# Inverse transform of two channels at a time, a second buffer for shifted rows, and the bias of three convolutions as one bf16 product

## What is computed

```python
xf = jnp.fft.fft2(x)                                  # per channel, 128x128
out_cplx = attention_of_heads(xf) @ xf                # out_f = abs(ifft2(out_cplx))
g = sigmoid(conv1x1(relu(bn(conv1x1(xf.real)))))
out_f_l = jnp.abs(jnp.fft.ifft2(g * xf))
fsa = conv1x1(concat([out_f, out_f_l]), projf_w)
t = conv1x1(x, w1x1, b1x1)                            # q, k and v each
q = concat([grouped_conv3(t), grouped_conv5(t)])      # zero padding of t, bias and all
out_s = softmax(l2norm(q_heads) @ l2norm(k_heads)) @ v_heads
out_s_l = concat([grouped_conv3(x), grouped_conv5(x)])
x = x + fsa + conv1x1(concat([out_s, out_s_l]), projs_w)
```

## Time and profile before

| | us |
|---|---|
| median of 3 runs | 28056.89 (28052.81 to 28061.12) |
| the profiled execution | 28067.24 |
| its span in the profile | 28065.3 |
| layer 0, eight images | 207 to 14546 of the span |
| layer 1 | 14546 to 28065 |
| TensorE busy | 24978.7 (89%) |
| VectorE busy | 19607.1 (70%) |
| ScalarE busy | 13778.0 (49%) |
| GpSimd busy | 12334.4 (44%) |

### The profile page before, as it was taken

How to read it: one execution, slowest core, us unless ns; L and a number is a source line. 1 busy time by engine, 2 the same in 40 slices (tenths; PEclk the granted TensorE clock), 3 DMA queues, 4 the chain that set the end, 5 groups by cost and what they waited for, 6 DMA issues and landing times. The chain is left out here.

```text
span 28065.3 us, 339160 instructions
## 1 busy us (share of the span) xinstructions
PE 24978.7 (89%) x112751; PEld 14810.9 (53%) x112751; DVE 19607.1 (70%) x22312; ACT 13778.0 (49%) x19719; POOL 12334.4 (44%) x4613
## 2 busy tenths in 40 slices
PE   6988989989899899898988888888888888888888
PEld 4676766767767677576763333333333333333333
DVE  2462643625536255362569999999999999999999
ACT  1313213132141321412327777777777777777777
POOL 0000000000000000000019999999999999999998
PEclk7999989989899899998999999999999999999999
DMA  1121021110211202111124444444444444444444
GB/s 51 47 69 61 18 60 53 59 58 23 64 58 44 59 29 71 58 36 59 36 106 168 166 189 167 186 170 165 188 168 189 167 188 167 168 189 165 189 167 164
DMA packets 816296, 3112.35 MB, mean 111 GB/s; under 512 B 61866, under 2 KB 325435, under 8 KB 530363
## 3 DMA queue, kind: packets, MB, share of 16 engines
q1 hardware_dynamic: 815802, 3105.94, 29.8%
HBM read 2813.42 MB, written 292.30 MB: 111 GB/s over the span
## 5 line engine op out<-in xcount | busy, mean ns | idle before, releaser
L2110 POOL TENSOR_TENSOR hid<-hid,bc 128x2048 f32<-128x2048 f32 x2048 | 7810.9, 3814 | 931.8 <-DVE carry L2016 929.6
L1779 PE MATMUL yp<-hid,ident 128*128 128x512 f32 x16384 | 7354.5, 598 | 439.0 <-POOL hid L2110 439.0
L2084 POOL TENSOR_SCALAR_AFFINE_SELECT ident<-ident 128x128 f32<-128x128 f32 x1 | 0.3, 292 | 14546.4 <-DVE ident L1969 14546.4
L1779 PEld LDWEIGHTS yp<-hid,ident 128*128 128x128 f32 x16384 | 3042.8, 189 | 4644.0 <-issue 3959.5
L2002 DVE TENSOR_TENSOR_SCAN hid<-da,carry,t 128x512 f32<-128x512 f32 x3968 | 4858.1, 1266 | 111.1 <-DVE carry L2016 11.5
L2008 DVE TENSOR_TENSOR_SCAN hid<-t,carry,hid 128x512 f32<-128x512 f32 x3968 | 4828.6, 1259 | 27.9 <-ACT t L1850 27.2
L2103 POOL TENSOR_TENSOR hid<-bc,du 128x1024 f32<-128x1024 f32 x2048 | 4097.2, 2001 | 192.4 <-PE yp L1779 164.8
L1005 PE MATMUL bk<-region 128*128 128x256 f16 (+2 forms) x32688 | 3872.1, 276 | 24.1 <-ACT region L1302 19.2
L1005 PEld LDWEIGHTS bk<-region 128*128 128x128 f16 (+2 forms) x32688 | 3296.3, 116 | 622.9 <-issue 196.5
L1850 ACT ACTIVATE t<-delta,v_a 128x512 f32<-128x512 f32 x4096 | 2659.5, 681 | 1569.9 <-DVE hid L2008 1566.7
L1735 PE MATMUL pj<-xn,w_x 128*128 128x512 f32 x4096 | 2379.4, 735 | 1071.0 <-ACT xn L1875 1023.5
(11 more groups left out here) (248 smaller groups left out, 26585.4 us busy)
## 6 DMA issues: line engine op xcount, KB each, us to landing
bc<-bc_rows SPq DMA_DIRECT2D x1024, 2048.0 KB, 7.2
work<-in_shift_d SPq DMA_DIRECT2D x256, 512.0 KB, 3.6
xpad<-in_x SPq DMA_DIRECT2D x32, 2048.0 KB, 19.0
work<-in_x SPq DMA_DIRECT2D x128, 512.0 KB, 5.3
gated<-work SPq DMA_DIRECT2D x256, 256.0 KB, 2.3
region<-gated SPq DMA_DIRECT2D x256, 256.0 KB, 2.9
region<-heads SPq DMA_DIRECT2D x256, 256.0 KB, 3.1
region<-in_x SPq DMA_DIRECT2D x256, 256.0 KB, 3.6
```

Of the source, the lines that this page charges most:

```text
L1779: m = nc.tensor.matmul(yp[:, h, :], ident[:, :], hid[:, k % 4, n, :], start=False, stop=(g == G - 1 and n == 3), skip_group_check=True)
L2110: nc.gpsimd.tensor_tensor(hid[:, k % 4, :, :], hid[:, k % 4, :, :], bc[:, g, 1, :, :], ALU.mult).then_inc(s_hc.sem, 1)
```

## The change

Five things are changed, all in layer 0.

1. XR and XI keep 64 columns per channel. Column 64 goes to a small buffer, XLAST, with a copy of its own per step on ACT and DVE, and after the gate it is folded into column 0; the table `back` takes the two apart. So two channels are 128 columns.
2. `inverse1` uses the columns of two channels as weights: one pair of products for two channels. Channel 2p+q leaves 64 rows, its neighbour the other 64. ACT copies 128 rows, once a step. `inverse2` of an even step contracts over rows 0 to 63, of an odd step over rows 64 to 127. A step now holds every other channel of eight, and the store of y has a stride of two channels.
3. Two buffers `shifted`. In the rows loop mix of step kk-1 is issued after the turn of step kk+1, and squares and root come two steps late. `rows_loop` peels two steps at either end.
4. The bias products: `bias_ab` and `bias_v` are split into three bf16 parts, stacked in rows 0, 32 and 64, over `valid` in bf16, repeated three times; they contract over 96 rows. In `five` and in the output convolution one product of 512 columns serves points 0 and 5 and stands ahead of them. In `three` it stays at 256 columns. In the output convolution the products of y and heads are 512 columns wide and stand at the end of the unit, with the waits for their transfers.
5. The kernel split (L900, L901) is done point by point, in the order of use, and PE waits for each point and for the bias just ahead of its first use. Making the three parts of `bias_v` takes seven small DVE instructions more, `thrice` copies the bias to the three places by a product.

```diff
+    back = np.concatenate([wt * cos[:64], wt * sin[:64]], 1)
+    back[0, P:] = cos[64] / HW
...
+        def three_parts(link, to, rest):
+
+
+            link(nc.vector.tensor_copy(to, rest))
+            for i in range(2):
+                sign = [k["later"][0:96, i:i + 1]]
+                link(nc.vector.scalar_tensor_tensor(rest, to, sign[0], rest, ALU.mult, ALU.subtract))
+                link(nc.vector.tensor_scalar(rest, rest, -1.0, None, ALU.mult))
+                last = nc.vector.tensor_copy(to, rest)
+                if i == 0:
+                    link(last)
+            return last
...
-                    V.tensor_copy(XI[:, 4 * t:4 * t + 4, :], bk[4 + t % 2][:, 0:4 * HALF].rearrange("p (c u) -> p c u", u=HALF)).then_inc(s_xi.sem, 1)
+                    spectrum = bk[4 + t % 2][:, 0:4 * HALF].rearrange("p (c u) -> p c u", u=HALF)
+                    V.tensor_copy(XLAST[:, 1, 4 * t:4 * t + 4], spectrum[:, :, U64])
+                    V.tensor_copy(XI[:, 4 * t:4 * t + 4, :], spectrum[:, :, 0:U64]).then_inc(s_xi.sem, 1)
...
+                            V.tensor_tensor(XLAST[:, i, :], XLAST[:, i, :], gates[:, n_u, :], ALU.mult).then_inc(s_gx.sem, 1)
...
+                V.tensor_tensor(XR[:, :, 0], XR[:, :, 0], XLAST[:, 1, :], ALU.subtract).then_inc(s_gx.sem, 1)
+                V.tensor_tensor(XI[:, :, 0], XI[:, :, 0], XLAST[:, 0, :], ALU.add).then_inc(s_gx.sem, 1)
...
-                    dve.wait_ge(s_o.sem, s_o.at(b, kk))
-                    V.tensor_copy(shifted[:, 512:], bk[2][:, :]).then_inc(s_shi.sem, 1)
-                    if not first:
-                        add_squares(kk - 1)
...
+                    dve.wait_ge(s_o.sem, s_o.at(b, kk - 1))
+                    V.tensor_copy(shifted[par][:, 512:], bk[2][:, :]).then_inc(s_shi.sem, 1)
+                    if not (isinstance(kk, int) and kk < 2):
+                        add_squares(kk - 2)
...
                 MT_ = MM.rearrange("p (t o) -> p t o", o=P)
-                link(V.tensor_scalar(M16[:, 0], MT_, col(24), None, ALU.mult))
-                V.scalar_tensor_tensor(M16[:, 1], MT_, col(24), M16[:, 0], ALU.mult, ALU.subtract).then_inc(s_ms.sem, 1)
+                for k_ in SLOT:
+                    of_point = slice(5 * k_, 5 * k_ + 5)
+                    link(V.tensor_scalar(M16[:, 0, of_point], MT_[:, of_point], col(24), None, ALU.mult))
+                    V.scalar_tensor_tensor(M16[:, 1, of_point], MT_[:, of_point], col(24), M16[:, 0, of_point], ALU.mult, ALU.subtract).then_inc(s_ms.sem, 1)
                 link(V.tensor_scalar(pt_scaled, pt[:, 0:2, :], col(25), None, ALU.mult))
-                V.tensor_scalar(bias_v[:, :], bk[6][0:T5, 0:P], small[0:T5, 25:26], None, ALU.mult).then_inc(s_bvc.sem, 1)
+                rest = bias_rest[:, 0, :]
+                link(V.tensor_scalar(rest, bk[6][0:96, P:2 * P], small[0:96, 25:26], None, ALU.mult))
+                three_parts(link, bias_v[:, :], rest).then_inc(s_bvc.sem, 1)
 
...
-                    for c in range(2):
-                        o = bk[p % 2][0:HALF, c * 256:(c + 1) * 256]
-                        mm(o, XR[:, 2 * p + c, :], k["cs"], start=True, stop=False)
-                        m = mm(o, XI[:, 2 * p + c, :], k["sc"], start=False, stop=True)
+                    for q in range(2):
+                        o = bk[p % 2][:, q * 256:(q + 1) * 256]
+                        mm(o, pairs[0][:, 2 * p + q, :], k["cs"], start=True, stop=False)
+                        m = mm(o, pairs[1][:, 2 * p + q, :], k["sc"], start=False, stop=True)
...
-                    pe.wait_ge(s_z.sem, s_z.at(b, 2 * t + 2))
+                    pe.wait_ge(s_z.sem, s_z.at(b, t // 2 * 2 + 2))
                     pe.wait_ge(s_abs.sem, s_abs.at(b, t - 1))
-                    mm(bk[2 + t % 2][:, :], k["back"][:, 0:P], Z[0:HALF, t % 2, :, 0:P], start=True, stop=False)
-                    mm(bk[2 + t % 2][:, :], k["back"][:, P:], Z[0:HALF, t % 2, :, P:], start=False, stop=True).then_inc(s_i2.sem, 1)
+                    r = slice(64 * (t % 2), 64 * (t % 2) + 64)
+                    mm(bk[2 + t % 2][:, :], k["back"][r, 0:P], Z[r, t // 2 % 2, :, 0:P], start=True, stop=False)
+                    mm(bk[2 + t % 2][:, :], k["back"][r, P:], Z[r, t // 2 % 2, :, P:], start=False, stop=True).then_inc(s_i2.sem, 1)
 
...
-                    if t + 1 < NK:
-                        inverse1(2 * t + 2)
-                        inverse1(2 * t + 3)
+                    if t + 2 < NK:
+                        inverse1(t + 2)
                     inverse2(t)
...
+                def mix(kk, par):
+                    pe.wait_ge(s_shr.sem, s_shr.at(b, kk + 1))
+                    pe.wait_ge(s_shi.sem, s_shi.at(b, kk + 1))
+
+                    pe.wait_ge(s_os.sem, s_os.at(b, 2 * kk - 2))
+                    o_re, o_im = bk[3 + 2 * par][:, :], bk[4 + 2 * par][:, :]
+                    re, im = shifted[par][:, 0:512], shifted[par][:, 512:]
...
-                    pe.wait_ge(s_shr.sem, s_shr.at(b, kk + 1))
-                    pe.wait_ge(s_shi.sem, s_shi.at(b, kk + 1))
-
-                    pe.wait_ge(s_os.sem, s_os.at(b, 2 * kk - 2))
-                    o_re, o_im = bk[3 + 2 * par][:, :], bk[4 + 2 * par][:, :]
-                    re, im = shifted[:, 0:512], shifted[:, 512:]
...
-                    mm(o_im, mix_t[:, 1, :], re, start=False, stop=True).then_inc(s_o.sem, 1)
+                    if not first:
+                        mix(kk - 1, 1 - par)
 
                 pe.wait_ge(s_abs.sem, s_abs.at(b, NK))
                 turn(0)
-                chunk_loop(pe, body)
+                rows_loop(pe, body)
+                mix(NK - 1, 1)
...
-                        ends = k_ in (0, 5)
-                        m = point(group, k_, WB16, 5, VP[par], slice(2 * i, 2 * i + 2), 0, not ends)
-                        if ends:
-                            r = k_ // 5
-                            m = mm(slot(group, k_), bias_ab[:, 1, :], valid[:, vrow + r:vrow + r + 3:2, :], start=False, stop=True)
+                        if k_ == 0:
+                            mm(bk[3 * group + 2][:, :], bias_ab[:, 1, :], valid[:, vrow:vrow + 4, :], start=True, stop=False)
+                        m = point(group, k_, WB16, 5, VP[par], slice(2 * i, 2 * i + 2), 0, True, k_ not in (0, 5))
...
-                pe.wait_ge(s_bvc.sem, s_bvc.at(b, 1))
-                pe.wait_ge(s_ms.sem, s_ms.at(b, 1))
...
-                        for k_ in SLOT:
-                            ends = k_ in (0, 5)
-                            m = point(i, k_, M16, 5, VP[par], slice(2 * i, 2 * i + 2), 0, not ends)
-                            if ends:
-                                r = k_ // 5
-                                mm(slot(i, k_), bias_v[:, :], valid[:, vrow + r:vrow + r + 3:2, :], start=False, stop=False)
-                                if k_ == 0:
-                                    pe.wait_ge(syc[i], b * (8 * NK) + j * 16 + 16)
-                                mm(slot(i, k_), pt_scaled[:, 1, :], by_row(ych[i])[:, r], start=False, stop=False)
-                                if k_ == 0:
-                                    pe.wait_ge(sof[i], b * (8 * NK) + j * 16 + 16)
-                                m = mm(slot(i, k_), pt_scaled[:, 0, :], by_row(of[i])[:, r], start=False, stop=True)
+                        for place, k_ in enumerate(SLOT):
+                            if k_ == 0:
+                                if is_first(j) and i == 0:
+                                    pe.wait_ge(s_bvc.sem, s_bvc.at(b, 1))
+                                mm(bk[3 * i + 2][:, :], bias_v[:, :], valid[:, vrow:vrow + 4, :], start=True, stop=False)
+                            if is_first(j) and i == 0:
+                                pe.wait_ge(s_ms.sem, s_ms.at(b, place + 1))
+                            point(i, k_, M16, 5, VP[par], slice(2 * i, 2 * i + 2), 0, k_ not in (0, 5), k_ not in (0, 5))
+                        both = bk[3 * i + 2][:, :].rearrange("p (r t w) -> p r t w", r=2, t=2)
+                        pe.wait_ge(syc[i], b * (8 * NK) + j * 16 + 16)
+                        mm(both, pt_scaled[:, 1, :], by_row(ych[i]), start=False, stop=False)
+                        pe.wait_ge(sof[i], b * (8 * NK) + j * 16 + 16)
+                        m = mm(both, pt_scaled[:, 0, :], by_row(of[i]), start=False, stop=True)
...
-                    cp(Z[0:HALF, p // 2 % 2, 2 * (p % 2):2 * (p % 2) + 2, :], bk[p % 2][0:HALF, :].rearrange("p (c n) -> p c n", c=2)).then_inc(s_z.sem, 1)
+                    cp(Z[:, p // 2 % 2, 2 * (p % 2):2 * (p % 2) + 2, :], bk[p % 2][:, :].rearrange("p (c n) -> p c n", c=2)).then_inc(s_z.sem, 1)
```

179 lines of the change are left out of this document (107 added, 72 removed).

## The result

The changed kernel takes 26,848.95 us (median of 4 runs, 26,840.82 to 26,852.97) against 28,056.71 us before (4 runs). The ratio is 0.9569 with a 95% interval of 0.9553 to 0.9586: 4.3% less. The forecast was 26,800 us, range 26,630 to 27,000. The profiled executions' spans are 26,839.0 and 28,065.3 us.

What follows compares the result with a forecast made beforehand. TensorE was taken to bound nearly every layer 0 stage, waiting only in the rows loop. Terms 42.6 + 15 + 49 + 54 - 3 gave 157.6 us an image, 1255 in all after setup: 26,800 us, range 26,630 to 27,000.

Steps and rivals of the forecast that it cites:

- Inverse transform: Inverse transform: a step falls from 5.18 to 3.85 us, gaining 42.6 us an image, bounds 30 to 55.
- disputed term: Inverse transform: changing between products of 128 and 64 rows costs 0.40 us a step, in and out.
- Rival 1: Inverse transform and rows loop: the change of rows is free and the loop reaches 5.92 us; 26,640 us, chance 0.10.
- rival 3: Inverse transform and rows loop: the change of rows costs 0.8 us and the loop gains nothing; 27,020 us, chance 0.08.
- Rows loop: Rows loop: a second `shifted` buffer cuts the period from 6.63 to 6.15 us, gaining 15 us an image.
- bound of 5.92: Rows loop: without TensorE's 0.71 us wait for DVE's copy, 5.92 us of the 6.63 us period would be left.
- q and k: Convolution of q and k: cheaper bias products, the wide one at 0.22 us, gain 49 us an image.
- rival 4: Bias products: the wide bf16 product costs 0.86 us, like a float32 one; 27,170 us, chance 0.05.
- Output convolution: Output convolution: units fall from 13.43 to 11.93 us and the first two units gain too; 54 us an image.
- rival 2: Output convolution: DVE becomes the bound and each unit takes 12.4 us; 26,910 us, chance 0.10.
- Forward transform, Gram and gate: These stages: small extra copies and DVE work cost 3 us an image, between 0 and 8; weight loads stay at 0.23.
- rival 5: Gram products: reads 256 bytes apart collide, making the kernel slower; a load must reach 0.87 us; chance 0.02.

## Why the prediction was right, and where it was off

**Inverse transform: right.** 42.6 us were forecast for the image. From its first product to the first turn of the rows loop the first image moved from 170.0 to 125.6 us, 44.4. The disputed term, 0.40 for the change of rows, measured 0.39. It was taken from the output convolution's bias slots, and that it fits so well is partly luck: there 25 rows stood among 128, here 64 do. Of the 0.42 in such a slot, 0.11 stands in the products of y and heads behind the bias, 0.97 us (1973.82 to 1974.79) for two products of 0.43:

```profile
1973.82 1.13 PE L1005 MATMUL bk<-region,work 128*128 128x256 f32 x4
```

A bias product alone lost 0.27 in float32 and 0.20 in bf16, both with 25 rows among float16 products. The value was right for this stage; the reason given, float32 weights on the sides, fits, but no run varied the type or the row count alone. Rival 1's free change is refuted, rival 3's double price too.

**Rows loop: right in size, wrong in its bound.** 15 us were forecast, and from first turn to the first product of q and k it is 249.6 to 235.8 in the first image, 13.8, and 14.9 in the mean of the eight. The period of 6.15 is met (6.08 and 6.22), and the wait is where it was put, for ScalarE's work. The bound of 5.92, that is 6.63 less the wait of 0.71, was false: TensorE's own work is 5.66. The idle time printed in a row starts at a modelled end, so subtracting it leaves 0.26 of a period unseen. From starts alone it could nearly have been read, from these rows of the kernel before, which stand between the two of the earlier trace rows:

```profile
810.16 1.95 PE L1005 MATMUL bk<-work 128*128 128x128 f32 x16
811.95 0.60 PE L1128 MATMUL bk<-ctab,work 128*128 128x128 f32 x4
```

Mix is 806.63 to 810.16, 3.53, and shift 1.79; the turn is 0.43 from start to start where nothing waits behind it. That is 5.75; in the run without the root mix is 3.44, and the sum is the 5.66.

**q and k: right.** 49 forecast; the stage with the softmax moved by 47.1. The price of the wide bf16 product, 0.22, was taken from two narrow ones and is exactly that; rival 4 falls. (Its words "a quarter of the float32 rate" mean a quarter of the float32 price, 0.111 us against 0.43.)

**Output convolution: right.** 54 forecast, 56.0 measured. A unit is 11.83 where 11.93 was forecast. The wait for the bias was forecast as 2.5. It is 2.85 in four of the eight images and 0.13 to 0.16 in the other four, whose products run at the lower clock, and the bias is used at the same moment in all; from the last small product to the end of unit 0 it is 17.6 us where it was 23.3, a gain of 5.7 where 6 were forecast. Unit 1 took 12.0 us instead of 17.1 in the first image; the waits for transfers and the slow products went nearly altogether. But the 17.1 that I read was not typical: over the eight images unit 1 took between 14.3 and 17.2 us before, 15.8 in the mean, and 11.9 after, so 3.8 where I gave 4. Behind unit 1 DVE never held TensorE up, though only 0.2 us are left in every second unit, so rival 2 didn't come.

**Forward transform, Gram and gate: the step that failed.** I charged 3 us, with "a load in 60.8/260 = 0.23 us as before". The forward transform cost nothing at all (first image 101.8 to 100.7 us, the small copies lie under TensorE's products), but the loads are at 0.277, and that is 11.1 us an image, 89 us in all, and the whole term came out at 10, outside its range of 0 to 8. It is rival 5's mechanism at the size of 0.04 us a load instead of the 0.64 that it needs to decide the sign. The rival was weighed as all or nothing, and its small form was left out of the forecast.

**How near the total is, and how much of that is luck.** With 89 us more the forecast would have stood at 26,889. Between the profiled executions the gain is 1226 us where 1255 were forecast: the images give 43 less (5.4 each, the dear loads partly made good by the other stages), and 14 come back at the end and in layer 1, where nothing was changed. The medians differ by 1208, because the profiled execution before lies 10 us above its median and the one after 8 below. So the total, 49 us off, is nearer than the terms deserve by what the other stages gave back, some 22 us, and by the 14.

## What to carry to other kernels

Count a product's cost from start to start, in rows and types like those it will stand among, and add a term for a change between weights of different row counts, in and out together: 0.39 us here for float32 products of 64 rows among 128, 0.20 for a bf16 product of 25. If a contraction has 64 rows, either fill it up to 128 with zeros, or put two of them directly behind each other on the two halves, where they cost as much as one. When a layout changes, look at every reader of it: the distance of a strided read is a cost of its own, and 256 bytes was the worst of four. Before a shorter wait or a lower clock is given a price, ask which engine sets the next moment that counts: at the head of the output convolution VectorE did, and the clock cost nothing.

## What was not expected

- A weight load of 128 float32 values with its product, both read at a distance of 256 bytes, takes 0.277 us, at 260, 264 and 272 bytes 0.234, 0.240 and 0.232. Why 256 is dear, and which of the two reads is, no run shows.
- Two float32 products of 64 rows on different halves of the array run at the same time with no loss: four in 1.91 us against two in 1.91.
- Behind 7.6 us of idle TensorE ran its next 60 products at a granted clock of 0.79 and lost 1.6 us in them, in all eight images. Behind 2.5 us of idle it came back at 1.00 in four of eight images and at the lower clock in the others, and that cost nothing, since the bias was not ready.
